# A vision tower on one core: attention on smaller score tiles, with transposed outputs and another order of work

## The reference, cut to what matters

```
x   = layernorm(h)
q, k, v = split(x @ Wqkv + bqkv)            # 16 heads of 16
s   = q @ k.T / 4 + bias, upper triangle -inf
p   = softmax(s, axis=-1)                    # over 37 keys
h   = h + (p @ v) @ Wout + bout
```

## Time and profile before

| | us |
|---|---|
| median of 3 runs (1295.07 to 1299.74) | 1297.36 |
| the profiled execution, its own time | 1297.63 |
| its span in the trace | 1295.4 |
| PE busy | 1150.3 (89%) |
| DVE busy | 699.3 (54%) |
| ACT busy | 636.0 (49%) |
| POOL busy | 444.9 (34%) |

### The profile page before, as it was taken

The page is one execution under the profiler, slowest core; times in us unless marked ns, Lnnn a source line. Parts: engine busy times, 40 slices in busy tenths (PEclk is TensorE's granted clock), DMA queues, the critical chain, the costliest instruction groups (busy, mean ns, idle before and its releaser), DMA issues.

```text
span 1295.4 us, 24968 instructions
## 1 busy us (share of the span) xinstructions
PE 1150.3 (89%) x8484; PEld 967.9 (75%) x8485; DVE 699.3 (54%) x1366; ACT 636.0 (49%) x1083; POOL 444.9 (34%) x334
## 2 busy tenths in 40 slices
PE   6989999989998887899999999961789998979998
PEld 5877777766676665788888888851567777769998
DVE  3257777663332324566666666620467767764443
ACT  3455555534333433455555555530465554535554
POOL 3255443513344533011122111113554555341110
PEclk9999999988998988899999999985899999989999
DMA  6550000007111112010111111103000000000000
GB/s 217 178 208 2 1 0 0 1 11 285 20 25 22 29 21 82 28 33 33 36 33 33 37 33 33 33 29 108 30 22 20 19 19 0 1 1 10 19 19 29
DMA packets 30786, 56.93 MB, mean 44 GB/s; under 512 B 12892, under 2 KB 22314, under 8 KB 29588
## 3 DMA queue, kind: packets, MB, share of 16 engines
q1 hardware_dynamic: 16184, 44.06, 9.8%
q0 software_dynamic: 13328, 10.66, 3.1%
q10 hardware_dynamic: 1228, 1.59, 0.4%
HBM read 41.50 MB, written 14.67 MB: 43 GB/s over the span
## 4 chain that ended last, share of the span: by engine, by line
PE 67%; DVE 9%; POOL 8%; issue 6%; ACT 4%; DMA 4%; SPq 0%; DVEq 0%; POOLq 0%; ACTq 0%
PE ps L1174 26%; PE ps L1179 11%; PE ps L1181 10%; PE ps L1180 10%; POOL routed_in L444 6%; PE ps L1288 4%; DVE Sb L834 2%; DMA yg<-routed_out 2%; PE ps L1540 2%; DVE mx L832 2%; DVE Sb L829 2%; PE ps L1281 2%; POOL xn L378 1%; PE ps L1304 1%; ACT vts L593 1%
## 5 line engine op out<-in xcount | busy, mean ns | idle before, releaser
L372 POOL TENSOR_TENSOR Km<-KT,cst 128x592 f32<-128x592 f32 x128 | 156.0, 1250 | 101.5 <-ACT KT L593 93.7
L468 POOL DMA_INDIRECT routed_out<-yt,tile_to x43 | 65.4, 1521 | 289.9 <-DVE yt L1109 285.7
L1087 DVE TENSOR_TENSOR tile_w<-arena,tile_w 128x1408 fp32r<-128x1408 f32 x86 | 139.3, 1621 | 35.6 <-ACT tile_w L770 35.6
L1174 PE MATMUL ps<-arena,shared 128*128 x516 | 130.9, 395 | 1.0 <-ACT shared L766 1.0
L1179 PE MATMUL ps<-tile_w,xTs 128*128 128x352 f32 x344 | 120.0, 349 | 2.5 <-DVE xTs L1092 2.5
L770 ACT ACTIVATE tile_w<-arena 128x1408 fp32r x86 | 118.2, 1376 | 6.5 <-issue 6.5
L926 DVE TENSOR_TENSOR Hd<-Sg,ps 128x296 f32<-128x296 f32 x96 | 44.4, 462 | 137.2 <-ACT Sg L711 134.0
L378 POOL TENSOR_TENSOR xn<-cen,rsd 128x592 f32<-128x592 f32 x32 | 46.7, 1460 | 192.8 <-ACT rsd L565 192.7
L1181 PE MATMUL ps<-tile_w,xTs 128*128 128x352 f32 x344 | 112.0, 326 | 0.0
L1174 PEld LDWEIGHTS ps<-arena,shared 128*128 128x128 f32 x516 | 90.9, 189 | 28.3 <-issue 15.6
L1180 PE MATMUL ps<-tile_w,xTs 128*128 128x352 f32 x344 | 111.7, 325 | 0.0
(11 more groups left out here) (199 smaller groups left out, 2816.6 us busy)
## 6 DMA issues: line engine op xcount, KB each, us to landing
arena<-in_ew_dram SPq DMA_DIRECT2D x7, 2176.0 KB, 13.2
x_in<-in_xT_dram SPq DMA_DIRECT2D x7, 888.0 KB, 5.2
xt<-routed_in SPq DMA_DIRECT2D x43, 129.0 KB, 2.1
yg<-routed_out SPq DMA_DIRECT2D x8, 592.0 KB
out_dram<-h SPq DMA_DIRECT2D x8, 296.0 KB, 2.7
routed_in<-zero_x SPq DMA_DIRECT2D x13, 129.0 KB, 4.6
gu_i<-in_gu_dram SPq DMA_DIRECT2D x1, 1536.0 KB, 20.7
shared<-in_gu_dram SPq DMA_DIRECT2D x1, 1408.0 KB, 7.5
```

The lines of the kernel that those rows point to most:

```text
L372: ins = pool.tensor_tensor(Km[p % 2][:, c], src, headmask.unsqueeze(2).to_broadcast([P, HG, W2]), ALU.mult)
L468: pool.indirect_dma_start(ys, bass.IndirectOffsetOnAxis(tile_to[b][:, 0:1], 0), yt[b][:], None).then_inc(s_yt, 16)
L1087: dve.tensor_tensor(tile_w[half][1], gate_up_of(w, half), tile_w[half][0].bitcast(F32), ALU.subtract).then_inc(s.wl, 1)
L1174: return pe.matmul(out_, lhsT, rhs, start=start, stop=stop)
```

## The change

Heads are masked in fours: HG is 4, Km is 128x592 for both chunks together, and the columns of Wq and Wk are permuted so that a 64-row half of a chunk holds four heads. `scores` becomes eight matmuls of 148 columns, on four 64x64 quarters. Rows of Pr are 37 long, not 64. `outputs` now has Vb as the stationary operand and writes the result transposed, 32 channels to a column quarter, so `outputs_t`, `out_t` and the small `lower_out` go. The reciprocals are written 16 times over (once per channel of a head, 128x256), transposed by two TensorE transposes at the head of `outputs`, copied by ScalarE (`shares_t`) and multiplied in `normalise`. Upper and lower halves of the result are made once per group, on ScalarE (`upper_out`) and GpSimd (`lower_out`). Zeroing of pads goes. V's copy is two masked activations per chunk. K is projected ahead of Q. Norms are two groups ahead; `softmax_in` is split into `scaled` and `centred`, and `scaled` runs one pair earlier.

```diff
-HG = P // HD
+HG = 4
...
+R64 = P // 2
+HW = HG * T
...
-        PTs = [carve(f"PTs{b}", HP, 2, T) for b in range(2)]
+        PTs = [carve(f"PTs{b}", HP, W2, rows=W2) for b in range(2)]
+        RTs = [carve(f"RTs{b}", DK, W2) for b in range(2)]
+        rs = [carve(f"rs{b}", HEADS, HD) for b in range(2)]
+        OTn = [carve(f"OTn{b}", DK, N) for b in range(2)]
...
         used[0] = both
+        xa.append(halves("xa1", DK, N))
...
+
+
+            return (F[l], 0) if X.near else (A[l], g + 2)
...
+
+                n = 4 * g + p
                 pool.wait_ge(a.S_mm, n + 1)
-                for c in range(DK):
-                    src = KT[:, c, p * W2:(p + 1) * W2].unsqueeze(1).to_broadcast([P, HG, W2])
-                    ins = pool.tensor_tensor(Km[p % 2][:, c], src, headmask.unsqueeze(2).to_broadcast([P, HG, W2]),
-                                             ALU.mult)
-                ins.then_inc(a.km, 1)
+                if p == 0:
+                    pool.wait_ge(a.proj, FREE + 6 * g + 2)
+                src = KT[:, :, p * W2:(p + 1) * W2].unsqueeze(2).to_broadcast([P, DK, HG, W2])
+                pool.tensor_tensor(Km[p % 2], src, headmask.unsqueeze(1).unsqueeze(3).to_broadcast([P, DK, HG, W2]),
+                                   ALU.mult).then_inc(a.km, 1)
+
+            def lower_out(a, g, gb):
+
+                pool.wait_ge(a.OTh, g + 1)
+                pool.tensor_tensor(OTs[1], OTn[gb], OTs[0].bitcast(F32), ALU.subtract).then_inc(a.OTs, 1)
...
-                if l == 1:
...
+                def step(g, b, X, turn):
+                    km(a, g, 3)
+                    if not X.first:
+                        lower_out(a, g - 1, 1 - b)
+                    if X.last:
+                        return
+                    km(a, g + 1, 0)
+                    if turn is not None:
+                        sum_routed(g + 3, 1 - b, turn)
+                    km(a, g + 1, 1)
+                    norm(*norm_ahead(l, g, X), b)
+                    km(a, g + 1, 2)
+                    if not X.near:
+                        lower_x(a, g + 2, b, xa[b])
+                    elif l == 1:
...
+                step(GROUPS - 1, 1, last, None)
+                lower_out(a, GROUPS - 1, 1)
                 if l == 1:
 
                     pool.wait_ge(C.h, 2 * GROUPS)
...
-                                   bias=qkv_b[:, k:k + 1] if l == 0 else zero_t[:]).then_inc(a.proj, 1)
+                        c = k - 2 * DK
+                        for odd in range(2):
+                            ins = act.activation(VT[:, c, :, odd], src.rearrange("p (i t) -> p i t", t=T), ACT.Identity, scale=vmask[:, odd:odd + 1],
+                                                 bias=val_b[:, c, odd:odd + 1] if l == 0 else zero_t[:])
+                        ins.then_inc(a.proj, 1)
 
...
-
-                def out_t(n, p, bk):
-
-                    act.wait_ge(a.OT_mm, FREE + n + 1)
+                    src = ps[0:W2, 4:6, :].rearrange("p b (h i q) -> p (b h) i q", h=HP // 2, i=2)[:, :, :, 0:T]
+                    act.activation(PTs[p % 2].rearrange("p h (i q) -> p h i q", i=2), src, ACT.Copy).then_inc(a.PTs, 1)
+
+                def shares_t(n, p, bk):
+
+                    act.wait_ge(a.O_mm, FREE + n + 1)
+                    act.wait_ge(a.OTn, n + 1)
                     src = ps[:, bk, 0:DK * P].rearrange("p (c i q) -> p c i q", c=DK, i=2)[:, :, :, 0:T]
-                    dst = OTs[0][:, :, p * W2:(p + 1) * W2].rearrange("p c (i q) -> p c i q", i=2)
-                    act.activation(dst, src, ACT.Copy).then_inc(a.OTh, 1)
...
-                        src = ps[rows, bk, :].rearrange("p (r w) -> p r w", w=2 * HD)[:, :, cols]
...
+                def step(g, b, X):
                     n = 4 * g
+                    if not X.first:
+                        shares_t(n - 1, 3, 6)
+                    values(n, 0, 7)
+                    probs_t(n, 0)
                     values(n + 1, 1, X.bank("V1"))
-                    probs_t(n, 0)
                     if not X.first:
...
-                    squares(*next_norm(l, g, X))
+                        upper_out(g - 1, 1 - b)
...
-                    values(n + 2, 2, X.bank("V2"))
+                    if not X.last:
+                        project(g + 1, 0, X.bank("proj0"))
+                        project(g + 1, 1, X.bank("proj1"))
+                    exps(n + 1, 1)
...
+                    halves_of = lambda t: t.rearrange("p (r h) k -> p r (h k)", r=2)
+                    dve.scalar_tensor_tensor(out=halves_of(Sb[b]), in0=ps[:, 2 * b:2 * b + 2, 0:DK * HW], scalar=HD ** -0.5,
+                                             in1=halves_of(bias[l][:]), op0=ALU.mult, op1=ALU.add).then_inc(a.sb, 1)
+
+                def centred(n, p):
...
                 def sums(n, p):
                     b = p % 2
                     dve.wait_ge(a.ex, FREE + n + 1)
-                    dve.tensor_reduce(sm[b][:], Pr[b][:, :, 0:T], AX_X, ALU.add).then_inc(a.sum, 1)
+                    dve.tensor_reduce(sm[b][:], Pr[b], AX_X, ALU.add).then_inc(a.sum, 1)
+                    dve.wait_ge(a.O_mm, n + 1)
                     dve.wait_ge(a.sum, FREE + n + 1)
-                    dve.reciprocal(rs[b][:], sm[b][:]).then_inc(a.rs, 1)
-
-                def normalise(n, p, bk):
-                    b = p % 2
-                    dve.wait_ge(a.O_mm, FREE + n + 1)
-                    dve.wait_ge(a.rs, FREE + n + 1)
-                    dve.wait_ge(a.OT_mm, n + 1)
-                    for i in range(2):
-                        r = slice(i * PITCH, i * PITCH + T)
-                        ins = dve.tensor_tensor(On[b][r].rearrange("p (h d) -> p h d", d=HD),
-                                                ps[r, bk, 0:D].rearrange("p (h d) -> p h d", d=HD),
-                                                rs[b][r].unsqueeze(2).to_broadcast([T, HEADS, HD]), ALU.mult)
-                    ins.then_inc(a.On, 1)
-
-                def lower_out(n, p, bk):
-
-                    dve.wait_ge(a.OTh, n + 1)
-                    cols = slice(p * W2, (p + 1) * W2)
-                    src = ps[:, bk, 0:DK * P].rearrange("p (c i q) -> p c i q", c=DK, i=2)[:, :, :, 0:T]
-                    upper, lower = [t[:, :, cols].rearrange("p c (i q) -> p c i q", i=2) for t in OTs]
-                    dve.tensor_tensor(lower, src, upper.bitcast(F32), ALU.subtract).then_inc(a.OTs, 1)
+                    dve.reciprocal(rs[b], sm[b][:].unsqueeze(2).to_broadcast([P, HEADS, HD])).then_inc(a.rs, 1)
+
+                def normalise(g, n, p, gb, bk):
+                    dve.wait_ge(a.RTs, FREE + n + 1)
+                    if p == 0:
+                        dve.wait_ge(a.OTs, g + 1)
+                    dve.tensor_tensor(OTn[gb][:, :, p * W2:(p + 1) * W2],
+                                      ps[:, bk, DK * P:DK * (P + W2)].rearrange("p (c q) -> p c q", c=DK), RTs[p % 2],
+                                      ALU.mult).then_inc(a.OTn, 1)
...
+                dve.wait_ge(a.xn, FREE + 1)
+                centre(a, 1, 6)
+                scaled(0, 0)
+                centred(0, 0)
+
+                def step(g, b, X):
                     n = 4 * g
-                    if l == 1 and not X.last:
-                        add_routed(g + 1, 0, X.bank("comb0"))
-                        add_routed(g + 1, 1, X.bank("comb1"))
+                    scaled(n + 1, 1)
...
+                        normalise(g - 1, n - 1, 3, 1 - b, 6)
+                    if X.comb:
+                        add_routed(g + 2, 0, X.bank("comb0"))
+                        add_routed(g + 2, 1, X.bank("comb1"))
                     sums(n, 0)
-                    normalise(n, 0, X.bank("O0"))
-                    softmax_in(n + 2, 2)
-                    if not X.first:
+                    centred(n + 1, 1)
+
+                    scaled(n + 2, 2)
+                    normalise(g, n, 0, b, X.bank("O0"))
+                    if not X.last:
+                        centre(*norm_ahead(l, g, X), X.bank("mean"))
+                    else:
                         residual(g - 1, 0, X.bank("out0p"))
                         residual(g - 1, 1, X.bank("out1p"))
                     sums(n + 1, 1)
...
+                    centred(n + 2, 2)
...
+                    scaled(n + 3, 3)
+                    normalise(g, n + 1, 1, b, X.bank("O1"))
+                    if not X.first and not X.last:
+                        residual(g - 1, 0, X.bank("out0p"))
                     sums(n + 2, 2)
...
                     for c in range(DK):
-                        for i in range(2):
-                            o = ps[i * PITCH:(i + 1) * PITCH, 2 * (p % 2) + c, :].rearrange("p (h k) -> p h k", k=PITCH)
-                            q0 = (2 * p + i) * T
-                            ins = mm(o[:, :, 0:T], QT[:, c, q0:q0 + PITCH], Km[p % 2][:, c, :, i * T:(i + 1) * T])
+                        for r in range(2):
+                            for i in range(2):
```

(46 more changed lines are left out.)

380 lines of the change are left out of this document (180 added, 200 removed).

## The result

The changed kernel takes **1434.69 us** (median of 3 runs, 1430.59 to 1434.92) for 1297.36: a ratio of 1.1048 [1.1004, 1.1092]. It is slower, as forecast, but by 137 us and not by 65.

The account below looks back on a forecast made before the run. TensorE bounded attention before; after, a loop through TensorE, VectorE and ScalarE would. First layer +24.7 and +3.9, second +28.1 and +8.6 make +65.3 on 1297.63: 1363 us, range 1284 to 1410 for 8 in 10.

Parts of the forecast that it names:

- The loop: Attention's body groups: TensorE, VectorE and ScalarE wait on each other in turn; a group takes 30.7 us, 33.7 with routed results.
- place 1: Second of a body group's four turns, from one transposing of exponentials to the next, with mean and centring; 8.3 us.
- The reciprocal: VectorE's reciprocal, now 128x256, takes 1.83 us, 1.75 to the next instruction, from a slope of 6.6 ns per element.
- The short rival: VectorE's long reciprocal costs like any other operation, 0.34 us instead of 1.75; 1293 us in all, chance 0.18.
- The quarters: TensorE's score matmuls on four quarters overlap, taking 0.65 us a turn; rival without overlap 1390 or 1453 us, chance 0.08.
- The last groups: Last attention group of each layer: +3.9 us in the first, +8.6 in the second, with TensorE waiting 7.7 for GpSimd.
- What was costed at nothing: The layers' starts and the kernel's start, where GpSimd's zeroing goes or was hidden behind the first load; +0 us.
- the clock as a rival: TensorE's idling halves its clock, doubling 2.5 us of its loop work in one turn of four; 1401 us, chance 0.10.
- the second of the prediction's own signs of being wrong: The forecast would be wrong if TensorE's granted clock left 1.00 in the body.
- places 2 and 3: Third and fourth turns of a body group, with output projection and residual in place of mean and centring; 8.0 us each.
- Contention at 0.9 us a group: VectorE's subtraction is held up by GpSimd, 0.23 us a turn, 0.9 a body group.
- VectorE as the fullest engine: A sign expected in the profile after: VectorE the fullest engine of the stretch.

Follow-up runs that it names:

- sums_first: Changed kernel with VectorE's sums and long reciprocals moved ahead of centring, residual and routed sum in each turn; 1315.76 us, ratio 1.0157.
- pool_early: Changed kernel with GpSimd's two subtractions for gu_lo and dn_lo moved ahead of the last lower_out; 1427.09 us.
- filled: Changed kernel with extra repeats of TensorE's V transposes, share transposes and projection 5 where TensorE stood still; 1426.12 us, ratio 1.0984.
- all3: Changed kernel with sums and reciprocals first, 16-element reciprocal plus spreading copy, and gu_lo and dn_lo before the last lower_out; 1290.94 us, ratio 0.9954.
- either change alone: Against 1290.94 us: VectorE's maximum ahead of centring, residual and routed sum, 1298.63; or ScalarE's exponentials ahead of projections' copies, squares and deviation, 1289.97; together 1274.76.

## Why the prediction was right in direction and wrong in size

- **The loop: right.** TensorE waits for ScalarE's exponentials, VectorE for means and projections, and place 1 came out at 8.6 us against 8.3 (0.3 too short, without contention). sums_first takes sums and reciprocal out of that chain and 119 us come back. That is more than the 65 that the loop alone was to cost, because the clock comes back with it.
- **The reciprocal: right.** 1752 ns for 1830. The short rival (1293 us) is out. The slope of the earlier trace rows held about: here it is (1752 - 253)/240 = 6.2 ns for each further element. The estimate of eight passes, from the repeat count of 8 that the Trainium skill gives (VectorE: DVE Perf Modes, "First, the fixed hardware budget"), had made 2.13 us; the measurement decides against it.
- **The quarters: right.** 0.65 for the scores. The outputs, kept at 1.11, take about 0.5 (their record is 0.48 long); they stand outside the chain.
- **The last groups: right.** +4.1 for +3.9, +10.3 for +8.6; the wait for dn_lo is 6.9 us for 7.7, and pool_early removes it (5.4 us net).
- **What was costed at nothing, the starts and the stretches between and behind the layers: 6.2 us too low in all** (2.4, 2.1 and 1.7 in the table's rows). No run was made for these.
- **The failed step: the clock as a rival "in one turn of four", at a chance of 0.10.** The forecast put TensorE's blocks in every turn, transposes 0.88, scores 0.65, mean or projection about 1, at a granted clock of 1.00. It was 0.86 and 0.82, the second of the prediction's own signs of being wrong. In the group of 34.55 us places 0 and 1 are near the forecast; places 2 and 3 are 10.3 and 9.8 where 8.2 each stood, contention included. Of those 3.6 us, 2 x 1.5 are TensorE's transposes, scores and projections at 1.2 GHz inside the loop (3.94 for 2.42 us ahead of the residual), 0.2 is contention above its share (the subtractions of 1.39 and 0.79), and 0.4 is the chain, which is 0.2 a turn too short at the full clock as well (from the transposes to the residual it takes 2.88 in the group before, where 2.65 was forecast). In the second layer's group of 40.22, which was forecast at 33.7, it is all four turns; VectorE's waits there are below.

```profile
1060.68 0.46 DVE L890 TENSOR_TENSOR h<-h,ps 128x296 f32 x1 [3.50 <-PE ps L1351]
1071.59 0.77 DVE L837 TENSOR_TENSOR cen<-h,ps 128x592 f32<-128x592 f32 x1 [4.05 <-PE ps L1201]
1081.27 0.53 DVE L883 SCALAR_TENSOR_TENSOR h<-ps,out_b,h 128x296 f32 x1 [3.68 <-PE ps L1208]
1091.29 0.53 DVE L883 SCALAR_TENSOR_TENSOR h<-ps,out_b,h 128x296 f32 x1 [3.62 <-PE ps L1208]
```

In turns at a granted clock of 0.97 or more these waits are 2.56, 2.51, 2.42 and 2.42 (the first from filled, at 1099.20): 4.9 us longer in all, of the 6.5 by which this group missed. My price for a turn at the low clock (2.5 us) was too high and the share of such turns far too low: in 37 of the 56 turns of these groups the granted clock was under 0.95, and 37 x 1.5, an estimate, is 56 of the 64 us missed. The earlier trace rows already had a stretch in which TensorE waited between its blocks, at 0.50, and the forecast's own loop made it wait in three turns of four.

- **Contention at 0.9 us a group: right in the first layer, low in the second.** The subtraction's mean is 986 ns there, 4 x (986 - 776) = 0.8; in the second layer's seven groups it is 1161, 1.5 a group, 4.5 us over all of them.

- **VectorE as the fullest engine: wrong.** TensorE is busy 176.92 us of the first stretch and VectorE 152.56; at the low clock the same work of TensorE takes longer.

What stays open: how the 64 us divide exactly, since clock and collision trade places when either is changed (filled), and why place 2 of the first layer keeps the full clock in some groups (8.7 to 8.8 us) and not in others (10.0 to 10.3).

## What to carry to other kernels

Read the new order of every queue as a loop before anything else: an operation that is 1.5 us longer cost 33 us where one turn in four held it and 58 to 80 us where all did (with what it did to the clock), and moving sums and reciprocal ahead in each turn gave back 119 us without removing any work. Where the forecast makes TensorE wait in nearly every turn of a loop that passes through it, price its blocks in that loop at both clocks and let the range hold both. Which of them it will be these runs don't tell beforehand: the kernel after stood still 78 us ahead of the exponentials and 63 ahead of the shares and ran at 0.86 and 0.82, all3 stood still 64 and 6 us at the same places and ran at 0.99 and 0.98 in its seven groups. Move an instruction forward only into time in which its engine stands still, and look at both queues that can hold the next step: here either change alone gave next to nothing and the two gave 16 us.
